# One product set for both comparison sides, five on-chip moves, and two copies in new places

## The chip, the cores and the metric

One core of a Trainium2 chip runs the whole program. The metric is the device time of one execution in microseconds (us). Five engines work side by side, each through its own list of instructions in order, and they wait for each other only by semaphores: TensorE (PE, matrix products into the eight PSUM banks), VectorE (DVE), ScalarE (ACT), GpSimd (POOL) and SyncE (SP), which here only issues transfers.

## The reference, cut to what matters

Eight sequences of 512 rows and 256 columns go through two layers. The first (causal attention with rotary positions beside an int8 projection) is not touched. The second is, for each of the eight sequences (a batch below):

```
xn    = layernorm(x)
left  = xn @ compare_left          # 256 -> 64
right = xn @ compare_right         # 256 -> 64
c     = left @ right.T / 16        # 512 x 512
g     = (c > threshold) * softmax(c + gate_bias)
attn  = g @ xn
xr, xk = two mixes of xn with xn moved down by one row, weights mu_r, mu_k
r     = sigmoid(xr @ W_r.T)
k     = square(relu(xk @ W_k.T))
out   = x + attn + r * (k @ W_v.T)
```

## The kernel before

Products are made in float16 pairs: a float32 value is split into a high part (its float16 copy) and a low part (what the copy left over), and three products, high by high, high by low and low by high, stand for one float32 product. Each split takes two passes: an engine copies (the high part), another subtracts (the low part).

The first layer runs as one long software pipeline over heads. The second runs batch by batch, as a pipeline written out by hand: each engine has a function `body3(n, u)` that lists its work of one turn, on batch n and on batches n+1 and n+2, and calls it for n = -1 to 7 (ACT from -2). The lists fix the order on each engine; nothing is scheduled at run time. One turn lasts some 20.6 us in the middle of the layer.

The work of a batch that the change touches or leans on, by function (engine, line):

- `turn` (PE, L1849): transposes the normalised rows `xn3` into banks 2 and 3. ACT copies them to `xt3h` (L940) and `xf3` (L947), DVE subtracts to `xt3l` (L1477).
- `rows_high` (ACT, L926, its instruction L932): copies the normalised rows, 128x1024, to float16 (`xn3h`). `rows_low` (POOL, L669, L674) subtracts to `xn3l`. Both are operands of the product `av3`. `rows_low(n+1)` is the first instruction of POOL's turn n; behind it stand `mix_before(n+1, 3)` (L683) and the two `key_low(n, .)` (L707), whose results `value(n, 0)` on PE waits for.
- `sides` (PE, L1859): six products of 512 columns for the left side into bank 2, and six for the right side into bank 3. The host lays each comparison matrix out twice, so that the result has the 64 values in partitions 0 to 63 and again in 64 to 127.
- `side_high` (ACT, L949, L955), twice: the left bank to `ls3`, the right bank to `rh3`. `side_low` (DVE, L1479): the lower half of `ls3` becomes the left side's low part (L1485), `rl3` the right side's (L1487). So `ls3` holds high over low, and two products (`ls3` by `rh3`, `ls3` by `rl3`) make a tile of comparisons.
- `compare` (PE, L1871): the four 128x512 tiles of comparisons, in banks 2 and 3 in turn. `top` (DVE, L1495) takes row maxima, `top_bias` (ACT, L963, L966) makes the bias, `exp3` (ACT, L974) the exponentials, `gated` (DVE, L1503, L1504) their reciprocals and the threshold mask.
- `pt3` (PE, L1926) transposes the masked tiles into banks 0 and 1, `pt3_high` (ACT, L983) and `pt3_low` (DVE, L1512) split them, `av3` (PE, L1943) multiplies them with the rows, `final` (DVE, L1542, four tiles) adds the result to `x_sb`, and SP stores it (L557).
- `mix_before` (POOL, L683) and `mix_all` (DVE, L1520) make the four mixes, `mix_high` (ACT, L991) and `mix_low` (POOL, L690) split them. `receptance`, `value` (PE, L1885) and `key` (PE, the products of L1650) use them; `key_relu`, `key_square`, `key_high` (ACT, L1006, L1014, L1022), `gate_value` (DVE, L1530) and `add_gated` (POOL, L697, L700) carry their results on.

The end of PE's turn n is: `key(n+1, 1)`, the two `sides(n+2, .)`, `pt3(n+1, 0)` and `(n+1, 1)`, `receptance(n+1, 1)`, `compare(n+2, 0)` and `(n+2, 1)`, `av3(n+1, 0)`, `pt3(n+1, 2)` and `(n+1, 3)`, `value(n+1, 0)`, `av3(n+1, 1)`; then the next turn begins with its two `turn`s, `value(n+1, 1)`, `receptance`, `compare` twice, `av3`, `key`, `av3`.

Of the kernel before, what the change touches and what calls it, by code (L numbers as in the profile page):

```python
# [5 lines left out]
NB = 8  # L6
SQ = 512
# [36 lines left out]
def build(nc, x_d, weights_d, w8_d, bqk_d, vec_d, thr_d, gate_d, tab_d, out_d):  # L44
# [11 lines left out]
    with ctx:  # L56
# [156 lines left out]
        kk = carve(KT * SQ).rearrange("p (k s) -> p k s", k=KT)  # L213
        st3 = sb("st3", [P, NT, 6], f32)
# [101 lines left out]
        lrl_done = sem("lrl_done")  # L316
        mixt_done = sem("mixt_done")
# [120 lines left out]
        def _(sp):  # L438
# [113 lines left out]

            for b in range(NB):
# [182 lines left out]
        def _(act):  # L736
# [189 lines left out]
            def rows_high(n, par):  # L926

                if absent3(n):
                    return
                after(act, xn3_done, made(NT, n, NT - 1))  # L930
                after(act, av3_mm, made(4, n - 2, 3))
                act.activation(xn3h[par], xn3[n % 2], ACT.Copy).then_inc(xn3h_done, 1)  # L932

            def xt_high(n, k):

                if absent3(n):
                    return
                after(act, tr3_mm, made(2, n, k))
                after(act, lr_mm, made(2, n - 1, 1))
                act.activation(xt3h[:, k, :], banks[2 + k][:], ACT.Copy).then_inc(xt3h_done, 1)  # L940
# [8 lines left out]
            def side_high(n, s):  # L949

                if absent3(n):
                    return
                after(act, lr_mm, made(2, n, s))
                after(act, c_mm, made(4, n - 1, 3))
                act.activation((ls3, rh3)[s], banks[2 + s][:], ACT.Copy).then_inc(lrh_done, 1)  # L955
# [68 lines left out]
            def body3(n, u):  # L1024
# [41 lines left out]
        def _(dve):  # L1066
# [412 lines left out]
            def side_low(n, s):  # L1479

                if absent3(n):
                    return
                after(dve, lrh_done, made(2, n, s))
                if s == 0:
                    dve.tensor_tensor(ls3[L:P], banks[2][L:P, :], ls3[L:P], ALU.subtract).then_inc(lrl_done, 1)  # L1485
                else:
                    dve.tensor_tensor(rl3, banks[3][:], rh3, ALU.subtract).then_inc(lrl_done, 1)  # L1487
# [59 lines left out]
            dve.memset(xf3[:, :, 0:1], 0.0).then_inc(xf3_zero, 1)  # L1547

            def body3(n, u):
# [10 lines left out]
                gate_value(n, 1, u)  # L1560
                gated(n + 1, 2, 1 - u)
# [18 lines left out]
            side_low(0, 0)  # L1580
            side_low(0, 1)
            top(0, 0, 0)
            mix_all(0, 2)
# [14 lines left out]
        def _(pe):  # L1598
# [260 lines left out]
            def sides(n, s, *users):  # L1859

                if absent3(n):
                    return
                after(pe, xt3l_done, made(2, n, 1))
                bank_free(users)
                pairs = []
                for k in range(KT):
                    a, z = lr_h[:, k, s, :], lr_l[:, k, s, :]
                    pairs += [(a, xt3h[:, k, :]), (a, xt3l[:, k, :]), (z, xt3h[:, k, :])]
                product(banks[2 + s][:], pairs, lr_mm)

            def compare(n, i, *users):  # L1871
# [3 lines left out]
                after(pe, lrl_done, made(2, n, 1))  # L1875
# [41 lines left out]
            def pt3(n, j, par):  # L1917
# [3 lines left out]
                if j == 0:  # L1921
                    after(pe, pm3_done, made(4, n, 3))
                    after(pe, x1_done, 2 * NB)
                after(pe, pt3l_done, made(4, n, j - 2))
# [29 lines left out]
            def body3(n, u):  # L1954

                turn(n + 2, 0, (pm3_done, 4, n + 1, 0), (lrl_done, 2, n + 1, 0), (pm3_done, 4, n, 2),
                     (xt3l_done, 2, n + 1, 0))
                turn(n + 2, 1, (pm3_done, 4, n + 1, 1), (lrl_done, 2, n + 1, 1), (pm3_done, 4, n, 3),
                     (xt3l_done, 2, n + 1, 1))
# [3 lines left out]
                compare(n + 1, 3, (xt3l_done, 2, n + 2, 1), (pm3_done, 4, n + 1, 1))  # L1963
                av3(n, 2, u)
# [6 lines left out]
                sides(n + 2, 0, (pm3_done, 4, n + 1, 2), (xt3l_done, 2, n + 2, 0))  # L1971
                sides(n + 2, 1, (pm3_done, 4, n + 1, 3), (xt3l_done, 2, n + 2, 1))
# [3 lines left out]
                compare(n + 2, 0, (lrl_done, 2, n + 2, 0))  # L1976
                compare(n + 2, 1, (lrl_done, 2, n + 2, 1))
# [18 lines left out]
            compare(0, 0, (lrl_done, 2, 0, 0))  # L1996
            compare(0, 1, (lrl_done, 2, 0, 1))
            attended(NB - 1, 1, (2, 3, 4, 5, 6, 7), pj)
# [51 lines left out]
```

## Time and profile before

| | us |
|---|---|
| median of 3 runs (lowest, highest) | 1029.79 (1029.18, 1029.96) |
| the profiled execution | 1030.44 |
| its span, first to last instruction | 1028.6 |
| PE busy | 987.3 (96%) |
| DVE busy | 837.6 (81%) |
| ACT busy | 757.0 (74%) |
| POOL busy | 767.6 (75%) |
| transfers' share of 16 DMA engines | 31% |

The span is the stretch that the profiler saw; the execution's own time is 1.84 us longer. A busy share is an average over both layers. The first layer ends near 840 us, and the stretch from there to the end is what the change touches. In a timeline a start and a duration are given for each instruction or run of like instructions; products overlap in PE's pipeline, so the distance from one start to the next, not the duration, is what an instruction costs there.

### The profile page before, as it was taken

The numbers are of one execution on the slowest core, as the hardware profiler recorded it, in microseconds if no ns is written. First come the engines' busy times: TensorE is split into PE (matmuls) and PEld (weight loads), VectorE is DVE, ScalarE is ACT, GpSimd is POOL, SyncE is SP. The second block draws the span as 40 slices with busy tenths as digits, with TensorE's granted clock in tenths as the row PEclk, the third lists the DMA queues.
The fourth block names the chain that finished last, engine by engine and source line by source line (L and its number), as shares of the span: only waits on it lengthen the run. The fifth ranks groups of instructions, "written<-read, shape, count | busy, mean of one in ns | idle before, by whom it ended". The sixth has DMA issues, their size and how long they took to land.

```text
span 1028.6 us, 23734 instructions
## 1 busy us (share of the span) xinstructions
PE 987.3 (96%) x8004; PEld 678.5 (66%) x8004; DVE 837.6 (81%) x2271; ACT 757.0 (74%) x2014; POOL 767.6 (75%) x942
## 2 busy tenths in 40 slices
PE   5889989999999999999999999999999998999997
PEld 4556655766666666666666666666666665777776
DVE  7989988788878888887778877778778756998875
ACT  5989987567676677676667667676766766999994
POOL 4777668877878787878687778787877545878874
PEclk9999999999999999999999999999999999999999
DMA  8734535234333333343333333333333100000101
GB/s 273 240 110 129 153 103 163 82 120 124 113 106 93 114 93 93 94 119 100 102 93 118 108 95 94 113 94 92 99 103 98 32 1 1 22 22 22 42 22 42
DMA packets 99704, 98.71 MB, mean 96 GB/s; under 512 B 13312, under 2 KB 95360, under 8 KB 98944
## 3 DMA queue, kind: packets, MB, share of 16 engines
q1 hardware_dynamic: 99584, 97.19, 31.0%
q8 instruction: 65, 1.06, 0.5%
q14 instruction: 55, 0.45, 0.2%
HBM read 56.25 MB, written 40.90 MB: 94 GB/s over the span
## 4 chain that ended last, share of the span: by engine, by line
PE 69%; DVE 15%; ACT 7%; issue 4%; POOL 3%; DMA 2%; SPq 0%; DVEq 0%; ACTq 0%; POOLq 0%
PE bank L1650 22%; PE bank L1747 12%; PE bank L1733 12%; PE bank L1764 7%; PE bank L1721 6%; PE bank L1722 5%; DVE arena L1361 2%; PE bank L1943 2%; ACT arena L872 2%; DVE arena L1520 2%; PE bank L1885 2%; POOL arena L628 2%; DVE arena L1377 1%; DMA arena<-in_weights 1%; DVE x_sb L1542 1%
## 5 line engine op out<-in xcount | busy, mean ns | idle before, releaser
L628 POOL TENSOR_SCALAR arena<-arena,rc 128x128 f32<-128x128 f32 (+3 forms) x512 | 277.7, 560 | 178.8 <-DVE rc L1370 177.9
L872 ACT ACTIVATE arena<-arena,nm 128x256 f32<-128x256 f32 (+3 forms) x512 | 283.5, 554 | 112.0 <-DVE nm L1361 107.5
L1361 DVE CUSTOM_DVE_ANT_0 arena<-bank,mask_rows 128x256 f32<-128x256 f32 (+3 forms) x512 | 232.8, 483 | 88.0 <-PE bank L1722 82.9
L1733 PE MATMUL bank<-ident,arena 128*128 128x128 f32 x1280 | 212.0, 278 | 12.4 <-DVE arena L1377 5.1
L1733 PEld LDWEIGHTS bank<-ident,arena 128*128 128x128 f32 x1280 | 149.8, 141 | 72.2 <-DVE arena L1377 29.8
L1722 PE MATMUL bank<-arena 128*128 128x256 f16 (+3 forms) x512 | 152.9, 299 | 0.0
L1747 PE MATMUL bank<-arena 128*64 128x512 f32 (+3 forms) x1024 | 152.0, 439 | 0.0
L1721 PE MATMUL bank<-arena 128*128 128x256 f16 (+3 forms) x512 | 139.9, 300 | 1.7 <-DMA arena<-scr 1.7
L1747 PEld LDWEIGHTS bank<-arena 128*64 128x64 f32 x1024 | 67.8, 136 | 94.8 <-issue 69.8
L1377 DVE COPY arena<-bank 128x512 f32<-128x512 f32 (+3 forms) x256 | 124.4, 486 | 3.7 <-PE bank L1733 3.3
L880 ACT ACTIVATE arena<-bank 128x512 f32<-128x512 f32 (+3 forms) x256 | 108.3, 423 | 15.1 <-PE bank L1733 14.4
L1650 PE MATMUL bank<-xsh,wh 128*128 128x512 f16 x256 | 97.2, 380 | 3.1 <-DVE wl L1203 2.4
L1764 PE MATMUL bank<-wh,arena 128*128 128x256 f16 x512 | 99.7, 273 | 0.4 <-DVE arena L1411 0.4
L1650 PE MATMUL bank<-xsh,wl 128*128 128x512 f16 x256 | 97.0, 379 | 0.0
L1650 PE MATMUL bank<-xsl,wh 128*128 128x512 f16 x256 | 97.0, 379 | 0.0
L890 ACT ACTIVATE arena<-bank,bvs 128x512 f16<-128x512 f32 x64 | 43.9, 687 | 71.5 <-PE bank L1747 71.3
L872 ACT ACTIVATION_READ_ACCUMULATOR arena<-arena,nm 128x1 f32 x512 | 96.1, 188 | 0.0
L1650 PE MATMUL bank<-wh,xsh 128*128 128x128 f16 x512 | 89.1, 219 | 1.7 <-DVE arena L1352 1.7
L1650 PE MATMUL bank<-wl,xsh 128*128 128x128 f16 x512 | 89.1, 219 | 0.0
L1650 PE MATMUL bank<-wh,xsl 128*128 128x128 f16 x512 | 89.1, 219 | 0.0
L600 POOL TENSOR_TENSOR arena<-arena 128x512 f32<-128x512 f32 x64 | 81.6, 1274 | 5.5 <-DVE arena L1352 5.4
L602 POOL TENSOR_TENSOR arena<-arena 128x512 f32<-128x512 f32 x64 | 83.0, 1297 | 0.0
(183 smaller groups left out, 2200.7 us busy)
## 6 DMA issues: line engine op xcount, KB each, us to landing
arena<-scr SPq DMA_DIRECT2D x320, 128.0 KB, 2.7
scr<-arena SPq DMA_DIRECT2D x256, 128.0 KB, 1.7
arena<-in_weights SPq DMA_DIRECT2D x5, 1024.0 KB, 7.7
x_sb<-in_x SPq DMA_DIRECT2D x8, 512.0 KB, 9.1
out<-x_sb SPq DMA_DIRECT2D x16, 256.0 KB, 2.2
xscr<-arena SPq DMA_DIRECT2D x12, 256.0 KB, 3.1
xsh<-xscr SPq DMA_DIRECT2D x6, 256.0 KB, 3.4
xsl<-xscr SPq DMA_DIRECT2D x6, 256.0 KB, 3.7
```

Source lines behind the costliest of these rows:

```text
L602: pool.tensor_tensor(r_o, t_es, t_oc, ALU.add).then_inc(r1_done, 1)
L628: last = pool.tensor_scalar(pr[slot][:, OFF[i]:OFF[i + 1]], pr[slot][:, OFF[i]:OFF[i + 1]], rc[:, slot, i:i + 1], 1.0, ALU.mult, ALU.mult)
L872: act.activation(pr[slot][:, OFF[i]:OFF[i + 1]], pr[slot][:, OFF[i]:OFF[i + 1]], ACT.Exp, scale=-1.0, bias=nm[:, slot, i:i + 1], accum_out ...
L880: act.activation(ptf[h][:, TOFF[j]:TOFF[j + 1]], (pt0, pt1)[h][:, 0:P * (NT - j)], ACT.Copy).then_inc(ptf_done[h], 1)
L1361: dve.tensor_tensor_reduce(pr[slot][:, OFF[i]:OFF[i + 1]], s_tile[i], mask_rows[:, SQ - P * (i + 1):SQ], -1.0, -MASKED, ALU.add, ALU.min, ...
L1377: dve.tensor_copy(ptf[1][:, TOFF[j]:TOFF[j + 1]], pt1[:, 0:P * (NT - j)]).then_inc(ptf_done[1], 1)
L1650: last = pe.matmul(out, lhs, rhs, start=(a == 0), stop=(a == len(pairs) - 1))
L1721: pe.matmul(out, q, kd[par][:, hh, 0:(i + 1) * P], start=True, stop=False)
L1722: last = pe.matmul(out, q, kz[par][:, hh, 0:(i + 1) * P], start=False, stop=True)
L1733: last = pe.transpose(banks[5 + h][:, (i - j) * P:(i - j + 1) * P], pr[2 * par + h][:, OFF[i] + j * P:OFF[i] + (j + 1) * P], ident[:])
L1747: last = pe.matmul(ob[h * L:(h + 1) * L, j * P:SQ], vf[:, j, h * L:(h + 1) * L], ptf[h][:, TOFF[j]:TOFF[j + 1]], start=(j == 0), stop=(j = ...
L1764: last = pe.matmul(bank[:, t * D:(t + 1) * D], o[:, slot, rows], w[:, p, :], start=(p == 0 and a == 0 and t == 0), stop=(p == NP - 1 and a ...
```

## The change: what it does

- **sides**: one set of six products takes the 128 weight columns that hold left and right once each, so that one bank has the left side in partitions 0 to 63 and the right side in 64 to 127. It goes to bank 0 (bank 2 for batch 0). On PE it moves from behind `key(n+1, 1)` to behind `compare(n+1, 3)`, ahead of `av3(n, 2)`.
- **side_high, side_low**: one instruction each on the whole bank, into two strips of dead weight space (`side_h`, `side_l`). On ACT `side_high(n+2)` now stands ahead of `top_bias(n+1, 1)`, on DVE `side_low(n+2)` ahead of `gated(n+1, 2)`.
- **move_sides**: SP moves the halves to where `compare` wants them, three transfers of 64 partitions behind `side_high` and two behind `side_low`. `compare` waits for all five. The lower half of `rl3` is set to zero once, so the product of the two low parts is left out.
- **rows_high**: the copy of the rows goes from ACT (behind `key_relu(n+1, 0)`) to DVE, behind `final(n, .)` and ahead of `mix_all(n+2, 2)`. POOL's list does not change.
- `pt3(n+1, 0)` also waits until `side_low(n+2)` has read bank 0; the start of the layer is reordered to match.

```diff
+            def move_sides(n):
+                after(sp, lrh_done, made(1, n))
+                for dst, src in ((ls3[0:L], side_h[0:L]), (rh3[0:L], side_h[L:P]), (rh3[L:P], side_h[L:P])):
+                    sp.dma_start(dst, src).then_inc(lr_moved, 16)
+                after(sp, lrl_done, made(1, n))
+                for dst, src in ((ls3[L:P], side_l[0:L]), (rl3[0:L], side_l[L:P])):
+                    sp.dma_start(dst, src).then_inc(lr_moved, 16)
+            move_sides(0)
+            move_sides(1)
             for b in range(NB):
+                move_sides(b + 2)
                 for u in range(2):
...
-                act.activation((ls3, rh3)[s], banks[2 + s][:], ACT.Copy).then_inc(lrh_done, 1)
+                after(act, lr_mm, made(1, n))
+                after(act, lr_moved, 80 * n)
+                act.activation(side_h, banks[0 if n else 2][:], ACT.Copy).then_inc(lrh_done, 1)
...
ACT body3:
                     normalised(n + 3, (0, 1))
+                side_high(n + 2)
                 top_bias(n + 1, 1, 1 - u)
                 exp3(n + 1, 2, 1 - u)
                 exp3(n + 1, 3, 1 - u)
                 key_relu(n + 1, 0)
-                rows_high(n + 2, u)
                 key_square(n + 1, 0)
                 key_high(n + 1, 0)
-                side_high(n + 2, 0)
                 key_relu(n + 1, 1)
-                side_high(n + 2, 1)
...
+            def rows_high(n, par):            # now on DVE
+                after(dve, xn3_done, made(NT, n, NT - 1))
+                after(dve, av3_mm, made(4, n - 2, 3))
+                dve.tensor_copy(xn3h[par], xn3[n % 2]).then_inc(xn3h_done, 1)
+            def side_low(n):
+                after(dve, lrh_done, made(1, n))
+                dve.tensor_tensor(side_l, banks[0 if n else 2][:], side_h, ALU.subtract).then_inc(lrl_done, 1)
...
DVE body3:
                 gate_value(n, 1, u)
+                side_low(n + 2)
                 gated(n + 1, 2, 1 - u)
                 gated(n + 1, 3, 1 - u)
                 mix_all(n + 2, 0)
                 mix_all(n + 2, 1)
                 final(n, 0, u)
                 final(n, 1, u)
+                rows_high(n + 2, u)
                 mix_all(n + 2, 2)
-                side_low(n + 2, 0)
-                side_low(n + 2, 1)
                 pt3_low(n + 1, 0)
...
+            lr_hf = wh[:, C_LR:C_WR].rearrange("p (k c) -> p k c", k=KT)[:, :, L:3 * L]
+            def sides(n, *users):
...
                 for k in range(KT):
+                    pairs += [(lr_hf[:, k], xt3h[:, k, :]), (lr_hf[:, k], xt3l[:, k, :]), (lr_lf[:, k], xt3h[:, k, :])]
+                product(banks[0 if n else 2][:], pairs, lr_mm)
             def compare(n, i, *users):
-                after(pe, lrl_done, made(2, n, 1))
+                after(pe, lr_moved, 80 * (n + 1))
...
PE body3:
                 compare(n + 1, 3, (xt3l_done, 2, n + 2, 1), (pm3_done, 4, n + 1, 1))
+                sides(n + 2, (pt3l_done, 4, n, 2))
                 av3(n, 2, u)
                 key(n + 1, 0, (er_done, 2, n + 1, 0))
...
                 key(n + 1, 1, (y3a_done, 2, n, 1))
-                sides(n + 2, 0, (pm3_done, 4, n + 1, 2), (xt3l_done, 2, n + 2, 0))
-                sides(n + 2, 1, (pm3_done, 4, n + 1, 3), (xt3l_done, 2, n + 2, 1))
                 pt3(n + 1, 0, 1 - u)
...
start of the layer, PE:
-            sides(0, 0, (xt3l_done, 2, 0, 0))
-            sides(0, 1, (xt3l_done, 2, 0, 1))
+            sides(0, (xt3l_done, 2, 0, 0))
             attended(NB - 1, 0, (4, 5, 6, 7), wo)
-            attended(NB - 1, 1, (0, 1), pj)
+            attended(NB - 1, 1, (0, 1, 2, 3), pj)
             compare(0, 0, ...)
```

## Rows read from the trace of the kernel before

**Rows 1.** Windows: start:end, length, then busy us (instructions) by engine, clock, DMA.

```profile
952.42:973.00 20.58, 20.40 (x154) 15.02 (x153) 16.97 (x32) 19.45 (x40) 16.91 (x16) 1.00 0.08 27
```

**Rows 2.** Timeline of PE: start us, duration us, line, operation, out<-in, count.

```profile
880.13 1.04 PE L1856 MATMUL bank<-ident,arena 128*128 128x128 f32 x8
881.00 0.38 PE L1885 MATMUL bank<-wh,arena 128*128 128x256 f16 x2
...
884.49 1.47 PE L1943 MATMUL bank<-arena 128*128 128x256 f16 x12
885.80 0.59 PE L1650 MATMUL bank<-arena,wh 128*128 128x512 f16 x2
...
950.25 0.59 PE L1650 MATMUL bank<-arena,wh 128*128 128x512 f16 x2
...
954.14 1.03 PE L1926 MATMUL bank<-ident,arena 128*128 128x128 f32 x8
...
959.62 0.38 PE L1885 MATMUL bank<-wh,arena 128*128 128x256 f16 x2
```

**Rows 3.** Timeline of ACT in the same stretch.

```profile
954.34 0.60 ACT L955 ACTIVATE arena<-bank 128x512 f16<-128x512 f32 x1
954.83 1.08 ACT L983 ACTIVATE arena<-bank 128x512 f16<-128x512 f32 x2
...
967.99 0.39 ACT L963 ACTIVATE arena<-nm,gate,sc_c 128x2 f32<-128x2 f32 x1
...
968.74 0.78 ACT L974 ACTIVATE arena<-bank,arena,sc_c 128x512 f32<-128x512 f32 x1
...
971.07 1.06 ACT L932 ACTIVATE arena<-arena 128x1024 f16<-128x1024 f32 x1
```

**Rows 4.** Timeline of DVE: a pair of mixes alone, and one turn.

```profile
888.92 1.40 DVE L1520 SCALAR_TENSOR_TENSOR arena<-arena,vec 128x512 f32<-128x512 f32 x2
...
952.42 1.65 DVE L1542 SCALAR_TENSOR_TENSOR x_sb<-bank,arena,x_sb 128x256 f32<-128x256 f32 x4
954.00 1.05 DVE L1520 SCALAR_TENSOR_TENSOR arena<-arena,vec 128x512 f32<-128x512 f32 x1
...
956.41 1.28 DVE L1512 TENSOR_TENSOR arena<-bank,arena 128x512 f16<-128x512 f32 x2
...
970.40 0.17 DVE L1503 RECIPROCAL arena<-arena 128x1 f32<-128x1 f32 x1
...
971.12 1.95 DVE L1520 SCALAR_TENSOR_TENSOR arena<-arena,vec 128x512 f32<-128x512 f32 x2
```

**Rows 5.** Timeline of POOL; in brackets idle before, and what ended it.

```profile
951.93 2.56 POOL L674 TENSOR_TENSOR arena<-arena 128x1024 f16<-128x1024 f32 x1
...
957.17 1.16 POOL L707 TENSOR_TENSOR arena<-arena 128x512 f16<-128x512 f32 x1 [0.43 <-ACT arena L1022]
...
968.04 1.36 POOL L683 TENSOR_SCALAR arena<-arena,omu 128x512 f32<-128x512 f32 x2
```

**Rows 6.** Groups of DVE by line and form: count, busy us, mean ns, idle before.

```profile
L1394 DVE TENSOR_TENSOR arena<-xsh,xsl 128x1024 f32<-128x1024 f16 x8 | 9.6, 1194 | 0.0
...
L1405 DVE TENSOR_SCALAR arena<-arena 128x1024 bf16<-128x1024 f32 x8 | 5.5, 688 | 0.0
```

**Rows 7.** All instructions of L674: ns least/median/most, first and last start us.

```profile
L674 POOL TENSOR_TENSOR arena<-arena x8: 2126/2560/2564, 850.0 to 993.1; 128x1024 f16<-128x1024 f32 x8
```

**Rows 8.** Timeline of PE: an early idle, and one at the layer's start.

```profile
28.93 0.38 PE L1650 MATMUL bank<-xsh,wh 128*128 128x512 f16 x1 [1.85 <-DVE wl L1203]
...
859.73 1.64 PE L1856 MATMUL bank<-ident,arena 128*128 128x128 f32 x8 [1.65 <-DVE arena L1504]
```

**Rows 9.** Windows just behind it, columns as in Rows 1.

```profile
862.00:864.00 2.00, 2.00 (x11) 1.37 (x9) 0.90 (x2) 1.04 (x4) 0.91 (x1) 0.50 0.00 0
```

**Rows 10.** The page's DMA issues: count, KB each, us from issue to landing.

```profile
arena<-scr SPq DMA_DIRECT2D x320, 128.0 KB, 2.7
```

**Rows 11.** Timeline of SP: two issues in the first layer.

```profile
798.01 0.90 SPq L515 DMA_DIRECT2D arena<-scr  x2
```

More of the change, by code:

```diff
@@ L924, in _ @@
                 ring(n)
[L926 to L932, printed above, removed]
             def xt_high(n, k):
@@ L938, in xt_high @@
                 after(act, tr3_mm, made(2, n, k))
-                after(act, lr_mm, made(2, n - 1, 1))
+                after(act, lr_mm, made(1, n - 1))
                 act.activation(xt3h[:, k, :], banks[2 + k][:], ACT.Copy).then_inc(xt3h_done, 1)
@@ L947, in xt_whole, with side_high @@
                 act.activation(xf3[:, k, 1:SQ + 1], banks[2 + k][:], ACT.Copy).then_inc(xf3_done, 1)
[L949 removed]
+            def side_high(n):
                 if absent3(n):
                     return
[L953 to L955 removed]
+                after(act, lr_mm, made(1, n))
+                after(act, lr_moved, 80 * n)
+                act.activation(side_h, banks[0 if n else 2][:], ACT.Copy).then_inc(lrh_done, 1)
             def top_bias(n, p, par):
@@ L1477, in xt_low3 @@
                 dve.tensor_tensor(xt3l[:, k, :], banks[2 + k][:], xt3h[:, k, :], ALU.subtract).then_inc(xt3l_done, 1)
-            def side_low(n, s):
+            def rows_high(n, par):
                 if absent3(n):
                     return
[L1483 to L1487, printed above, removed]
+                after(dve, xn3_done, made(NT, n, NT - 1))
+                after(dve, av3_mm, made(4, n - 2, 3))
+                dve.tensor_copy(xn3h[par], xn3[n % 2]).then_inc(xn3h_done, 1)
+            def side_low(n):
+                if absent3(n):
+                    return
+                after(dve, lrh_done, made(1, n))
+                dve.tensor_tensor(side_l, banks[0 if n else 2][:], side_h, ALU.subtract).then_inc(lrl_done, 1)
             def top(n, p, par):
@@ L1547, in _ @@
             dve.memset(xf3[:, :, 0:1], 0.0).then_inc(xf3_zero, 1)
+            dve.memset(rl3[L:P], 0.0).then_inc(rl3_zero, 1)
             def body3(n, u):
@@ L1579, in _ @@
             mix_all(0, 1)
-            side_low(0, 0)
-            side_low(0, 1)
+            side_low(0)
+            mix_all(0, 2)
+            rows_high(0, 0)
             top(0, 0, 0)
-            mix_all(0, 2)
             residual(NB - 1, 0, wo)
@@ L1857, in turn @@
                 last.then_inc(tr3_mm, 1)
-            def sides(n, s, *users):
+            lr_hf = wh[:, C_LR:C_WR].rearrange("p (k c) -> p k c", k=KT)[:, :, L:3 * L]
+            lr_lf = wl[:, C_LR:C_WR].rearrange("p (k c) -> p k c", k=KT)[:, :, L:3 * L]
+            def sides(n, *users):
                 if absent3(n):
@@ L1923, in pt3 @@
                     after(pe, x1_done, 2 * NB)
+                if j == 0 and not absent3(n + 1):
+                    after(pe, lrl_done, made(1, n + 1))
                 after(pe, pt3l_done, made(4, n, j - 2))
@@ L1954, in body3 @@
             def body3(n, u):
[L1956 to L1959, printed above, removed]
+                turn(n + 2, 0, (pm3_done, 4, n + 1, 0))
+                turn(n + 2, 1, (pm3_done, 4, n + 1, 1))
                 value(n, 1, (er_done, 2, n, 1))
@@ L1975, in body3 @@
                 receptance(n + 1, 1, (kr_done, 2, n + 1, 1))
-                compare(n + 2, 0, (lrl_done, 2, n + 2, 0))
-                compare(n + 2, 1, (lrl_done, 2, n + 2, 1))
+                compare(n + 2, 0, (pm3_done, 4, n + 1, 2))
+                compare(n + 2, 1, (pm3_done, 4, n + 1, 3))
                 av3(n + 1, 0, 1 - u)
```

19 lines of the change are left out of this document (13 added, 6 removed).

## The prediction

> **What bounds the kernel now.** I read the page's busy shares first (PE 96%), then the windows of the second layer one turn at a time, then each engine's timeline of one clean turn. In the turn from 952.42 to 973.00 us PE is busy 20.40 of 20.58 us, ACT 19.45, DVE 16.97, POOL 16.91 [rows 1]. PE is the bound, but by little: ACT has 1.1 us of air, and DVE and POOL, with 3.6 us each, sit in chains that reach PE only just in time. So a product set taken away is worth its time only if the chains that feed PE shorten with it. Those chains, not the busy shares, decide this change. The layer has six turns (n = 0 to 5) with all of the changed work, and its start.
>
> **What is removed.** A set of six products of 512 columns costs 1.30 us of PE: three such sets (a key and the two old sides) run from 950.25 to 954.14 [rows 2]. One set a batch goes: 8 x 1.30 = 10.4 us, if nothing takes its place. ACT loses one side copy (0.60) and the copy of the rows (1.06) a batch [rows 3]. On DVE the two old subtractions stood between the third mix and `pt3_low`, from 954.00 + 1.05 to 956.41, 1.36 us [rows 4]; one of some 0.7 us comes back in a place where DVE waits for the exponentials anyway, so I count it at nothing.
>
> **What is added.** (a) Five transfers of 64 partitions. The first layer's, of 128 KB, land 2.7 us after issue [rows 10] and are issued 0.45 us apart [rows 11]. In the turn worked out below, counted from `turn(n+2, 1)`, `side_high` ends at 6.0 and `side_low` 0.7 later, the last move is issued at 7.7 and lands at 10.4; `compare(n+2, 0)` comes at 12.6 at the earliest (5.23, five sets of 1.30 to 1.31: `av3`, `key`, `av3`, `key`, `receptance`, and the two `pt3` at 0.87). PE's queue behind that wait holds `av3(n+1, 0)` and the rest of the turn, but there are 2.2 us of cover, and I count it at nothing. SP's stores stand behind the moves of batch n+2, which are issued some 4 us before `final(n)` ends; they lose nothing. (b) The zeroing of half of `rl3`, once: a fraction of a microsecond beside a DVE that waits. (c) The copy of the rows on DVE. No such copy stands in the trace. The nearest row is a one-input pass over 1024 columns from float32 to a 16-bit type, 0.69 us; the other end is the two-input pass over 1024 columns, 1.19 us [rows 6]. I take 0.69, since the copy too has one input, and keep 1.19 for the range.
>
> **What is moved, and why it costs.** This is the point of the change that decides. The copy of the rows is not only work for DVE: POOL's `rows_low` waits for it, and behind `rows_low` on POOL stand `mix_before` and the two `key_low`, for which `value(n+1, 0)` on PE waits. Before, ACT had the copy done early (971.07 + 1.06 = 972.13, before POOL was free at 972.50), and the key's low part was ready at 957.17 + 1.16 = 958.33 for a `value` that began at 959.62 [rows 2, 3, 5]: 1.3 us of slack. Now the copy stands on DVE behind the mask of the last exponential, two mixes and four tiles of `final`. And the exponentials themselves now stand behind `side_high`, which waits for the new product set. That closes a loop through four engines. I add it up from the issue of `turn(n+2, 1)` on PE to that of `turn(n+3, 1)`:
>
> - PE: half of a pair of `turn`s, 0.44 (the pair takes 881.00 - 880.13 = 0.87); `value`, `receptance` and two `compare`s, 884.49 - 881.00 = 3.49; the new set 1.30 [rows 2]. Now 5.23.
> - ACT: `side_high` starts 0.20 behind PE's last product (954.34 against the next group's 954.14) and the next instruction 0.49 later [rows 2, 3]; now 5.92. The maxima have long been there (both `compare`s are through at 4.1, two maxima at 0.6 each give 5.4 at most), so `top_bias` starts. 0.75 to the third exponential, and 970.40 - 968.74 = 1.66 until DVE can mask the fourth [rows 3, 4]. Now 8.33.
> - DVE: the mask 0.72 (to 971.12); two mixes, `final` 1.58 (954.00 - 952.42) and the copy 0.69 [rows 4, 6]. The two mixes took 1.95 in the last turn, with POOL at work, and 1.40 alone; 0.08 of each overlaps what follows, so 1.87 or 1.32 [rows 4]. In the new order POOL is through with its list by about 8.7 and stands idle, waiting for the copy; I take 1.32. Now 12.64.
> - POOL: `rows_low` 2.56, the median (least 2.13) [rows 7]; one `mix_before` 0.68 (two took 1.36) and two `key_low` of 1.16 [rows 5]. With 0.05 at the hand-over, now 18.25.
> - PE: `value` and `av3` at 1.31 each (884.49 to 885.80), half a pair of `turn`s 0.44 [rows 2]. The loop closes at 21.3 us.
>
> PE's own work in a turn falls from at most 20.4 to 19.1 [rows 1], so it would stand still over 2 us a turn: first at `av3(n+1, 0)`, which it could begin at 13.5 (the 12.6 of its `compare`s and 0.87 for the two), while its `pt3_low` ends behind the copy and the third mix, at 12.6 + 1.05 + 0.68 = 14.3; then well over a microsecond at `value(n+1, 0)`. What is late next, if the POOL part were gone, is that same `pt3_low`, in a loop of some 19.6. So each of the six turns takes 21.3 instead of 20.58: +0.7 us each, +4.3 in all. The start gains: before the first `turn(1, .)` one set less stands ahead of the last first-layer products, whose residual the first mask waits for, so 1.3 us come off, and the first POOL chain keeps that gain (its turn had a slack of that size). The last turns have neither sides nor a copy and stay. Sum: 4.3 - 1.3 = +3.0 us on the profiled execution's 1030.44, which is 1033.4; that execution lies 0.65 above the median of the runs, so the median comes to **1033 us**.
>
> **A rule weighed against this.** The two mixes show what sharing costs: 1.95 beside a busy POOL, 1.40 beside an idle one [rows 4]; `rows_low` shows it from the other side, 2.13 or 2.56 [rows 7]. The Trainium skill (SBUF - State Buffer, on the port that VectorE and GpSimd share) says that a VectorE instruction with two SBUF inputs, or in a two-port mode, holds the shared port pair for its whole length and the other engine blocks fully. The trace agrees in size, an extra 0.43 to 0.55 us being most of one mix of 0.7 us. By that rule the third mix, issued right behind the copy, would be first at the port and `rows_low` would end after 0.7 + 2.13 us; by the row it is 2.56. The loop would be 21.5 by the rule against 21.3.
>
> **Rivals.**
> 1. *The same loop, and the clock falls in its stalls.* PE idled 1.65 us before 859.73, and its `turn`s then took 1.64 us in place of 1.04; behind them it ran at a granted clock of 0.50, the lower of its two levels (1.2 GHz), in the window to 864 [rows 2, 8, 9]. At half speed the sets of such a stretch cost twice as much: 1.31 more for one, and I count 1.7 us for each such fall. Stalls of 0.8 and over 1 us would come each turn. Against: an idle of 1.85 us before 28.93 [rows 8] left the clock at full, as did every other one of the trace. If it falls in three to six of the turns, +5 to +10 more: 1038 to 1043, nominal 1040.
> 2. *Faster: the chains overlap more than I think, and PE keeps the set's time.* If the `value` wait does not bind (the copy is issued early, or POOL's list runs ahead), the loop left is PE's own, 19.1 at most. Eight sets give up to 10.4: 1019.4, and 1024 if half of it is lost again in ACT's order. For it: ACT, the second busiest, loses 1.66 us a turn. Against: every link of the sum above is forced by the written order.
> 3. *No change:* the short ends throughout, `rows_low` 2.13, gives a loop of 20.85, +0.3 a turn, and 1030.3 with the start's gain; or one link of half a microsecond hidden. 1028 to 1032.
> 4. *The moves are late.* Only beyond 2.2 us of cover, and then PE's stalls at `av3` and `value` absorb two more; a landing of over 7 us would be needed. Each further microsecond costs 6. I give it 2 in 100 and fold it into the first.
>
> **How the numbers follow.** The forecast (the loop at full clock) 0.50; its own range is 1030 to 1041: the low end with `rows_low` at 2.13, the high end with the copy at 1.19, mixes at 1.87 and a `mix_before` beside a mix, 22.5 a turn. The clock rival 0.20, faster 0.17, no change 0.13. Range for 8 in 10: 1022 to 1042, which leaves out the best part of the faster case and the worst of the clock. Within 0.2% is what a measurement of this kernel can't tell from none, 2.06 us, 1027.7 to 1031.9: the no-change case and the forecast's low end, 0.18. Faster 0.18, slower 0.64.
>
> **What would show it.** In the new profile: the distance between two groups of `final` 21.3 instead of 20.6 us in six turns; PE waiting 1 to 2 us before `value`'s L1885 line, released by POOL's `key_low`; POOL idle 3 to 4 us before `rows_low`, released by DVE's copy; that copy at 0.69; transfers landed before `compare`. The prediction is wrong if `key_low` is done before `value` comes up, if the copy takes well over 1.2 us, if PE waits for a transfer, or if a turn falls below 20 us.

## The result, and the profile after

| | before | after |
|---|---|---|
| median of the runs, us | 1029.88 (1029.18 to 1030.99, 4 runs) | 1036.91 (1035.74 to 1038.96, 4 runs) |
| the profiled execution, us | 1030.44 | 1038.96 |
| its span, us | 1028.6 | 1037.1 |
| PE busy, us (share of the span) | 987.3 (96%) | 982.8 (95%) |

The ratio is 1.0067, interval 1.0047 to 1.0088: slower by 7.0 us. The forecast was 1033, range 1022 to 1042.

The time went into the turns. The first fence has windows of the new kernel's trace from one group of `final` to the next, columns as in [rows 1]; the three short windows below them are stretches in which PE's clock was low, two inside these turns and one in the turn behind them.

```profile
890.43:913.39 22.96, 20.89 (x148) 15.47 (x146) 17.80 (x39) 17.98 (x37) 16.08 (x15) 0.93 0.13 39
913.39:935.62 22.23, 19.61 (x148) 14.34 (x146) 20.60 (x37) 17.99 (x37) 16.01 (x15) 1.00 0.14 39
935.62:958.58 22.96, 20.89 (x148) 15.17 (x146) 20.78 (x38) 17.98 (x37) 16.03 (x15) 0.93 0.13 38
958.58:979.88 21.30, 19.24 (x148) 14.38 (x146) 16.20 (x31) 17.98 (x37) 16.08 (x15) 1.00 0.15 42
...
900.00:902.00 2.00, 2.00 (x12) 1.38 (x11) 1.83 (x3) 0.00 (x0) 1.58 (x3) 0.50 0.04 8
944.00:946.00 2.00, 2.00 (x11) 1.36 (x10) 1.90 (x6) 0.61 (x2) 1.52 (x2) 0.50 0.00 0
989.00:991.00 2.00, 2.00 (x11) 1.42 (x10) 1.01 (x2) 0.00 (x0) 1.00 (x2) 0.50 0.00 0
```

A clean turn takes 21.30 us and has 19.24 us of PE work in it, against 20.58 and 20.40 in [rows 1]. Three of the six take 22.96 with the clock at 0.93 on average (the third of them starts at 979.88), one takes 22.23 at full clock, and two are clean. At 900, 944 and 989 us PE runs at a granted clock of 0.50, its lower level of 1.2 GHz. Now the clean turn, DVE first (timeline, columns as in [rows 4]):

```profile
975.56 0.69 DVE L1500 TENSOR_TENSOR wh<-bank,wh 128x512 f16<-128x512 f32 x1 [0.27 <-ACT wh L965]
977.07 0.16 DVE L1516 RECIPROCAL arena<-arena 128x1 f32<-128x1 f32 x1 [0.81 <-ACT arena L984]
977.83 0.16 DVE L1516 RECIPROCAL arena<-arena 128x1 f32<-128x1 f32 x1
978.56 1.41 DVE L1533 SCALAR_TENSOR_TENSOR arena<-arena,vec 128x512 f32<-128x512 f32 x2
979.88 1.65 DVE L1555 SCALAR_TENSOR_TENSOR x_sb<-bank,arena,x_sb 128x256 f32<-128x256 f32 x4
981.45 0.68 DVE L1493 CAST arena<-arena 128x1024 f16<-128x1024 f32 x1
982.05 0.74 DVE L1533 SCALAR_TENSOR_TENSOR arena<-arena,vec 128x512 f32<-128x512 f32 x1
982.71 1.28 DVE L1525 TENSOR_TENSOR arena<-bank,arena 128x512 f16<-128x512 f32 x2
```

The copy of the rows (the CAST of L1493) takes 0.68 us, behind the mixes and `final`. What waits for it stands in POOL's and PE's timelines of the same turn:

```profile
982.22 2.56 POOL L692 TENSOR_TENSOR arena<-arena 128x1024 f16<-128x1024 f32 x1 [4.12 <-DVE arena L1493]
984.76 0.69 POOL L701 TENSOR_SCALAR arena<-arena,omu 128x512 f32<-128x512 f32 x1
985.42 2.26 POOL L725 TENSOR_TENSOR arena<-arena 128x512 f16<-128x512 f32 x2
987.74 0.39 PE L1905 MATMUL bank<-wh,arena 128*128 128x256 f16 x2 [1.93 <-POOL arena L725]
```

POOL stands idle for 4.12 us until the copy comes, then runs `rows_low` (2.56), `mix_before` and two `key_low`, and PE has stood idle 1.93 us when `value(n+1, 0)` can start. In the kernel before, `key_low` was ready 1.3 us before PE wanted it [rows 2, 5]. The view of PE's waits, from 880 to 1000 us (in total, times, longest), shows this as the only wait of weight:

```profile
PE bank L1905 <- POOL arena L725: 9.7, 5, 1.9
PE bank L1870 <- DVE arena L1517: 0.5, 1, 0.5
```

The transfers are not among them. The page's line that answers to [rows 10] is

```profile
arena<-wh SPq DMA_DIRECT2D x40, 64.0 KB, 2.0
```

**The account.** From `value(0, 0)` to `value(6, 0)`, six turns, the new kernel takes 133.7 us and the old one 123.2. The 10.5 us are six turns at 21.30 (127.8, so +4.6), three falls of the clock at 1.66 each (22.96 - 21.30; +5.0), and 0.93 for the turn of 22.23. The rest of the profiled execution's +8.5 is the first layer, which the change does not touch and which ended 1.6 us later in this execution, the start (-1.1 to the first `turn(1, .)`, and -1.0 behind it, where the old kernel had its one fall of the clock, [rows 9], and the new one has none), and -1.5 in the last turns. I don't count the 1.6 us of the first layer to the change. PE waits there for a transfer just ahead of 46 us, in every trace of this case and for 1.12 to 3.43 us (1.67 before, 2.35 in the changed kernel), and in five of the fourteen (the changed kernel and experiments 1, 5, 9 and 11) its clock then falls to 0.50; in experiments 7 and 8 it falls behind the next wait, near 55 us, and in the kernel before at neither. In these seven the second layer's first DVE instruction starts at 843.7 us or later, in the other seven at 843.5 or earlier, but for experiment 12 (844.8), whose wait was 3.28 us.

### The profile page after: what moved, and what is told of

Read it like the earlier page. It is cut to its first block, busy times and chain, and to the rows that moved or that the text cites. A ratio compares the mean times of both kernels' runs of the same rounds, so it can differ in the third digit from the quotient of the medians.

```text
span 1037.1 us, 23654 instructions
## 1 busy us (share of the span) xinstructions
PE 982.8 (95%) x7956; PEld 675.2 (65%) x7956; DVE 837.3 (81%) x2272; ACT 745.7 (72%) x1998; POOL 763.4 (74%) x942
## 4 chain that ended last, share of the span: by engine, by line
PE 67%; DVE 12%; POOL 7%; ACT 6%; issue 5%; DMA 2%; SPq 0%; POOLq 0%; DVEq 0%; ACTq 0%
PE bank L1664 20%; PE bank L1761 12%; PE bank L1747 11%; PE bank L1778 7%; PE bank L1735 6%; PE bank L1736 5%; DVE arena L1369 2%; PE bank L1905 2%; PE bank L1965 2%; POOL arena L646 2%; POOL arena L692 1%; DVE arena L1385 1%; ACT arena L890 1%; POOL arena L725 1%; DMA scr<-arena 1%
## 5 line engine op out<-in xcount | busy, mean ns | idle before, releaser
L898 ACT ACTIVATE arena<-bank 128x512 f32<-128x512 f32 (+3 forms) x256 | 108.5, 424 | 14.9 <-PE bank L1747 14.3
L1778 PE MATMUL bank<-wh,arena 128*128 128x256 f16 x512 | 99.7, 273 | 0.9 <-DVE arena L1419 0.9
```

Source lines behind the costliest of these rows:

```text
L898: act.activation(ptf[h][:, TOFF[j]:TOFF[j + 1]], (pt0, pt1)[h][:, 0:P * (NT - j)], ACT.Copy).then_inc(ptf_done[h], 1)
L1778: last = pe.matmul(bank[:, t * D:(t + 1) * D], o[:, slot, rows], w[:, p, :], start=(p == 0 and a == 0 and t == 0), stop=(p == NP - 1 and a ...
```

## Experiments

Each is compared with the kernel before on the same chip. "The changed kernel" is the one measured above.

**1. The copy alone, in the kernel before.**

```
  (ACT)                 key_relu(n + 1, 0)
-                       rows_high(n + 2, u)
  (DVE)                 final(n, 1, u)
+                       rows_high(n + 2, u)
                        mix_all(n + 2, 2)
```

> The kernel before with nothing changed but the copy of the rows, on DVE behind final. Theory (the copy's place and side_high ahead of the exponentials each add a part to the loop): the fourth exponential is masked 7.6 us after turn(., 1), not 8.3, but the mixes run beside a busy POOL, so the loop is 20.6 to 21.2 against 20.6: 1030 to 1034. Rival (the copy's place costs it all by itself): 1036 or more.

Measured: 1034.47 us (1031.96 to 1035.61), ratio 1.0039, interval 1.0025 to 1.0053. Three turns took 20.81 to 20.93 us, two 22.3. PE waited at three places, each only a little:

```profile
PE bank L1857 <- DVE arena L1503: 1.8, 2, 0.9
PE bank L1651 <- DVE arena L1486: 1.5, 5, 0.4
PE bank L1886 <- POOL arena L707: 1.1, 5, 0.2
```

So one line's move from ACT to DVE costs, with all the old products in place, over half of the change's loss (0.39% of 0.67%). The two long turns were expected by neither theory; they wait 0.9 us at `turn` for a mask (first line), and experiments 4 and 5 are about them.

**2. The change without the copy's move.**

```
  (ACT)                 key_relu(n + 1, 0)
+                       rows_high(n + 2, u)
                        key_square(n + 1, 0)
  (DVE)                 final(n, 1, u)
-                       rows_high(n + 2, u)
```

> The changed kernel with the copy of the rows back on ACT, behind key_relu(n+1, 0); all else as changed. Theory (the loop sides, side_high, exponentials, copy, rows_low, key_low, value sets the turn): POOL gets the copy 2.7 us earlier, value no longer waits for key_low, and a turn falls from 21.3 to 19.2 to 19.6 us, bound by PE and by pt3_low; with no long stall the clock stays at full. 1036.9 - 6 x 1.8 - about 5 for the clock: 1019 to 1023. Rival (the cost is in side_high ahead of the exponentials or in the transfers, not in the copy's place): at least 1032.

Measured: 1026.12 us (1025.42 to 1027.14), ratio 0.9962, interval 0.9947 to 0.9977: 10.8 us below the changed kernel, and faster than before. PE waits for POOL nowhere, the clock stays at 1.00, and the turns take 20.24 to 20.55 us, not the 19.2 to 19.6 expected. It lies between the two ranges expected. That the POOL chain carries the loss is shown; why a turn is still 1.0 us over PE's work is the matter of experiments 6 to 10.

**3. The copy on DVE, but ahead of the two mixes.**

```
  (DVE)                 gated(n + 1, 3, 1 - u)
+                       rows_high(n + 2, u)
                        mix_all(n + 2, 0)
                        ...
                        final(n, 1, u)
-                       rows_high(n + 2, u)
```

> The changed kernel with the copy still on DVE but ahead of mix_all(n+2, 0), so before two mixes and final. Same work on every engine. Theory (what counts is when the copy ends, not which engine makes it): the copy can start when av3(n, 3) is through, 2.4 us earlier than now; POOL's chain is then no longer last, pt3_low is, and a turn takes 19.6 us: 1021 to 1025. Rival (DVE's load is what costs): unchanged, 1035 to 1039.

Measured: 1039.03 us (1037.54 to 1039.78), ratio 1.0085, interval 1.0070 to 1.0100. A clear miss of the theory, by 14 us and in sign. The number is at the edge of the rival's (DVE's load, 1035 to 1039), but DVE has the same instructions as in the changed kernel; what is new is what they meet. The copy starts 9.9 us behind the pair of `turn`s in place of 12.4, so 2.5 us earlier, but now `rows_low` meets the two mixes (timeline):

```profile
978.58 0.69 DVE L1493 CAST arena<-arena 128x1024 f16<-128x1024 f32 x1 [0.28 <-PE bank L1965]
979.18 3.30 DVE L1533 SCALAR_TENSOR_TENSOR arena<-arena,vec 128x512 f32<-128x512 f32 x2
979.36 2.58 POOL L692 TENSOR_TENSOR arena<-arena 128x1024 f16<-128x1024 f32 x1 [1.16 <-DVE arena L1493]
982.40 1.65 DVE L1555 SCALAR_TENSOR_TENSOR x_sb<-bank,arena,x_sb 128x256 f32<-128x256 f32 x4
985.37 1.98 PE L1965 MATMUL bank<-arena 128*128 128x256 f16 x12 [2.39 <-DVE arena L1525]
```

The pair of mixes takes 3.30 us in place of 1.41, `final` and `pt3_low` come later by that, and PE waits 2.39 us at `av3(n+1, 0)`. Turns alternate between 21.45 us and, with a fall of the clock, 23.11. The rule that the forecast weighed (the Trainium skill, "SBUF — State Buffer", section "Who interferes with whom") speaks of an exclusive lock on the port that VectorE and GpSimd share; the trace agrees in size, since the excess of 1.89 us is most of a `rows_low` (2.13 at the least, [rows 7]). In the order of the changed kernel the same `rows_low` meets one mix at most, and that is 0.74 us.

**4. Spare products in the stall, and 5. the same with the roots moved.** Experiment 4 puts eight products of 512 columns, which nobody reads, ahead of `value(n+1, 0)`. Experiment 5 adds the edit below. `roots` are small DVE instructions (128x8) that take the inverse square root of the last two batches' variances, six at the end of each of two turns.

```
  (PE)                  pt3(n + 1, 3, 1 - u)
+                       keep_busy(n + 1)
                        value(n + 1, 0, (kr_done, 2, n + 1, 0))
  (DVE, experiment 5)   side_low(n + 2)
+                       if 1 <= n < 3:
+                           roots(last_two, 3, (2 * n - 2, 2 * n - 1))
                        gated(n + 1, 2, 1 - u)
                        ...
-               elif n < 3:
-                   roots(last_two, 3, (2 * n - 2, 2 * n - 1))
```

> The changed kernel with eight spare products of 512 columns (1.73 us, results thrown away) on PE in the place of its wait for key_low, in the turns that have the wait. Theory (the clock falls in some turns because PE stands still 1.93 us): no half-clock stretch any more, turns of 21.3 us throughout, 1031 to 1033.5. Rival (the long turns of 22.96 us have another cause): 1036 to 1039 as before.

> Base: the changed kernel with the spare products ahead of value (which keeps the clock at full rate), and in addition the root of the last two batches' variances taken not at the end of two turns, beside POOL's rows_low and key_low, but ahead of gated(n+1, 2), where DVE waits for the exponentials and POOL has no long pass. My theory (the two long turns, 22.23 and 22.30 us, come from these small DVE instructions, 1.0 us each beside POOL, which delay the next mask): all five turns 21.3, 1.9 us less than the filled kernel, 1033 to 1034 us. Rival (the two turns are long for another reason, or the instructions take as long in the new place): 1035 to 1036.

Experiment 4: 1035.50 us (1034.16 to 1035.84), ratio 1.0053, interval 1.0036 to 1.0070, with turns of 21.30, 22.23, 22.30, 21.30 and 21.30. The windows of three of them:

```profile
889.46:910.76 21.30, 20.96 (x156) 15.15 (x154) 17.79 (x40) 17.98 (x37) 16.09 (x15) 1.00 0.14 42
910.76:932.99 22.23, 21.34 (x156) 15.08 (x154) 20.60 (x38) 17.99 (x37) 16.01 (x15) 1.00 0.14 39
932.99:955.29 22.30, 21.33 (x156) 15.06 (x154) 20.67 (x38) 17.99 (x37) 16.02 (x15) 1.00 0.14 40
```

The loop is not shortened by the filling, and the clock stays at 1.00 throughout: the 22.96 turns were 21.30 plus what a fall costs behind a stall. (This is the fastest of four executions; the other three have a mean clock of 0.998, as the kernel before has with one fall, wherever it lies. Experiment 5's trace, filled too, has one fall in the first layer and none in the second.) The time stayed 2 us above what was expected, and two turns are 1.93 us longer together. In them DVE is busy 20.6 to 20.7 us, against 17.8 in the first line and 16.2 in the two that are not shown. DVE's timeline of the changed kernel shows what these hold, and that of the kernel before the same instructions:

```profile
919.03 1.08 DVE L1090 TENSOR_SCALAR nw<-nw 128x8 uint32<-128x8 uint32 x1
920.15 1.08 DVE L1092 TENSOR_SCALAR nw<-nw 128x8 int32<-128x8 int32 x1
921.26 1.01 DVE L1097 TENSOR_TENSOR nw<-nw 128x8 f32<-128x8 f32 x1
922.30 1.01 DVE L1099 SCALAR_TENSOR_TENSOR nw<-nw 128x8 f32<-128x8 f32 x1
923.35 0.17 DVE L1101 SCALAR_TENSOR_TENSOR nw<-nw 128x8 f32<-128x8 f32 x1
```

```profile
918.19 1.01 DVE L1082 TENSOR_SCALAR nw<-nw 128x8 uint32<-128x8 uint32 x1
919.24 0.17 DVE L1084 TENSOR_SCALAR nw<-nw 128x8 int32<-128x8 int32 x1
919.44 0.17 DVE L1089 TENSOR_TENSOR nw<-nw 128x8 f32<-128x8 f32 x1
```

An instruction on eight columns takes 0.17 us while POOL is idle and 1.0 to 1.1 us beside one of POOL's two-input passes of 512 columns; two pairs of such passes end at 921.20 and 923.29, and the second and the fourth of the long instructions 0.03 us or less behind them. Since POOL's list now runs later, four meet it in place of one, and the next mask is late.

Experiment 5: 1036.39 us (1034.96 to 1037.87), ratio 1.0053, interval 1.0032 to 1.0073: not the 1033 to 1034 hoped for. The turns took 23.00, 22.98 and three times 21.30. The extra time moved by one turn, together with the roots, so the roots are its cause. But ahead of `gated(n+1, 2)` there was no room either: they take 2.6 us there (931.02 to 933.64; two of the six still meet a pass of POOL, against what was expected), of which DVE's wait for the exponential hides 0.8 to 0.9, and 1.7 is seen.

**6 and 7. What holds the kernel of experiment 2: is it the wait for the sides?** Its turns of 20.3 us I put down to ACT's list, which waits 0.50 us for the sides. Both kernels start from experiment 2; in 6 the sides are split behind the exponentials again, in 7 DVE makes `side_high`.

```
  (ACT, 6)  -           side_high(n + 2)
                        top_bias(n + 1, 1, 1 - u)
                        exp3(n + 1, 2, 1 - u)
                        exp3(n + 1, 3, 1 - u)
            +           side_high(n + 2)
  (DVE, 6)  side_low(n + 2) behind gated(n + 1, 3, 1 - u)
  (DVE, 7)  +           side_high(n + 2)
                        side_low(n + 2)
```

> Base: the changed kernel with the copy of the rows back on ACT; and the sides split behind the exponentials again (side_high behind exp3(n+1, 3), side_low behind gated(n+1, 3)), the single product set and the transfers kept. Theory: what bounds the kernel with the copy on ACT (turns of 20.3 us) is ACT's own list with its 0.50 us of waiting for the sides; without that wait turns of 19.8 and 1023 to 1024 us. Rival: the sides come too late for the comparison (side_low behind the masks ends at 9 us, the moves land 2 us and their issues later, comparison at 12.6 with nothing to spare) or pt3 waits for the split, and the turn stays at 20.3 or more: 1026 or above.

> Base: the changed kernel with the copy of the rows back on ACT; and side_high (512 columns, 0.60 us) made by DVE right ahead of side_low instead of by ACT ahead of the exponentials. Theory (ACT's list with its wait for the sides sets the turn of 20.3 us): ACT loses 0.60 us and the wait of 0.50, DVE has 1.3 us of idle time at that place; turns of 19.3 to 19.5 and 1020 to 1022 us. Rival (DVE's masks come later by 0.6 us and with them the mixes, final and PE's receptance): turns of 20 to 20.3, 1025 to 1026.

Measured: 1025.92 us (1025.04 to 1026.95), ratio 0.9952, interval 0.9937 to 0.9967; and 1027.04 (1025.81 to 1027.71), ratio 0.9960, interval 0.9947 to 0.9973. Both have the turns of experiment 2 (20.24 to 20.60), and both the same wait of PE, six times 0.9 us, here that of experiment 6:

```profile
PE bank L1904 <- ACT arena L1024: 5.3, 6, 0.9
PE bank L1869 <- DVE arena L1518: 0.6, 2, 0.3
```

So my theory fell. L1904 is `receptance(n+1, 1)`, L1024 `key_relu(n+1, 1)`. In these kernels it costs nothing to split the sides ahead of the exponentials, nor does it matter which engine does it: the three ratios, 0.9962, 0.9952 and 0.9960, lie in each other's intervals.

**8, 9 and 10. The relu directly behind the copy.** Edit of 8, on experiment 2; 9 is the same on experiment 7, 10 on experiment 6.

```
  (ACT)                 rows_high(n + 2, u)
+                       key_relu(n + 1, 1)
                        key_square(n + 1, 0)
                        key_high(n + 1, 0)
-                       key_relu(n + 1, 1)
```

> Base: the changed kernel with the copy of the rows back on ACT (turns 20.3 us; PE waits 0.89 us in each at receptance(n+1, 1) for key_relu(n+1, 1)). Here key_relu(n+1, 1) stands directly behind the copy, ahead of the square and the high part of key 0. New theory: with the product set gone, the bound is a short loop av3(n, 3) on PE - copy of the rows (waits 0.54 to 0.68 for it) - square, high, relu on ACT - receptance on PE; it does not pass the sides, since moving or splitting them elsewhere left 0.89 us of that wait. With the relu 1.2 us earlier the wait goes and av3(n+1, 0) is the next, waiting 0.2 for its pt3_low: turns of 19.5 to 19.7, 1021 to 1023 us. Rival (ACT's list, 18.7 busy of 20.3, with its waits for PE sets the turn): the wait moves elsewhere, 1025 to 1026.

> As the kernel with the relu directly behind the copy, and side_high made by DVE ahead of side_low. Theory of the PE-ACT loop: PE-bound in both, so 0 to 0.3 us a turn better at most: 1020 to 1022 us. Rival (ACT's list bounds once the relu is early): this one is 0.5 to 1 us a turn faster than the one with side_high on ACT ahead of the exponentials, 1018 to 1020.

> As the kernel with the relu directly behind the copy, and the sides split behind the exponentials (side_high behind exp3(n+1, 3), side_low behind gated(n+1, 3)). This tells what splitting the sides ahead of the exponentials costs by itself once nothing else holds the turn: if the exponentials' wait for the sides (0.50 us on ACT) matters, this one is 0.3 to 0.5 us a turn faster, 1019 to 1021 us; if not, the two are within 0.1 us a turn, 1021 to 1023.

Measured: 1028.89 us (ratio 0.9987, interval 0.9976 to 0.9999), 1029.48 (0.9990, 0.9980 to 0.9999) and 1027.89 (0.9982, 0.9971 to 0.9993): some 3 us slower than without the edit, where 3 to 7 faster were expected. Experiments 8 and 10, which differ only in where the sides are split, are equal within their intervals. All three have turns of 20.5 to 20.6 us. Between experiments 2 and 8 that is only 1.0 us over the five middle turns; another 1.3 us lie in the last two, whose cause was not followed. The wait at `receptance` is gone, and the same time is waited at `turn` for the mask of the first exponential. The timeline of experiment 8, cut to the links of one turn:

```profile
951.30 1.06 ACT L950 ACTIVATE arena<-arena 128x1024 f16<-128x1024 f32 x1 [0.54 <-PE bank L1964]
959.79 0.78 ACT L992 ACTIVATE arena<-bank,arena,sc_c 128x512 f32<-128x512 f32 x1
960.69 0.16 DVE L1517 RECIPROCAL arena<-arena 128x1 f32<-128x1 f32 x1 [3.17 <-ACT arena L992]
961.65 1.39 PE L1869 MATMUL bank<-ident,arena 128*128 128x128 f32 x8 [0.87 <-DVE arena L1518]
970.26 1.47 PE L1964 MATMUL bank<-arena 128*128 128x256 f16 x12
971.83 1.06 ACT L950 ACTIVATE arena<-arena 128x1024 f16<-128x1024 f32 x1 [0.54 <-PE bank L1964]
```

Read in order of time it is a loop: the copy of the rows on ACT waits for `av3(n, 3)`, whose buffer it overwrites; from the copy ACT takes 9.4 us to the first exponential, DVE 1.0 us to its mask, and PE 10.2 us from `turn` to the next `av3(n, 3)`. The sum is 20.53 us, the turn. The timelines show 0.18 us of waiting within ACT's 9.4 us and none within PE's 10.2. Without the edit the loop is another through the same copy, in experiment 2's timeline:

```profile
969.54 1.06 ACT L950 ACTIVATE arena<-arena 128x1024 f16<-128x1024 f32 x1 [0.54 <-PE bank L1964]
971.69 0.67 ACT L1024 ACTIVATE arena<-bank,sc 128x512 f32<-128x512 f32 x1
972.50 0.38 PE L1904 MATMUL bank<-wh,arena 128*128 128x256 f16 x2 [0.89 <-ACT arena L1024]
```

It takes 2.96 us from the copy through square, high part and relu to `receptance`, and the other 17.3 of its 20.24 us are PE's, from there to the next `av3(n, 3)`. Both contain PE's new product set, which the change put ahead of `av3(n, 2)`; in the old order it stood behind `key(n+1, 1)`, outside the part from `turn` to `av3(n, 3)`. So the 1.3 us that PE saves a turn seem to be partly outside the loops that bind: that is read from the order and the traces, and no run isolates it. Whether another place for the set, or a third buffer for the copy, would free them was not tried.

**11. Experiment 7 with the roots of experiment 5.**

> The changed kernel with the copy of the rows on ACT, side_high on DVE, and the roots of the last two batches ahead of gated(n+1, 2). Theory: as the kernel with side_high on DVE, and up to 1 us less, if that one has turns lengthened by the roots at their old place; 1019 to 1022 us. Rival: DVE has no room left ahead of gated(n+1, 2) in those two turns, so it is 0 to 1 us slower than without the move.

Measured: 1035.43 us (1031.99 to 1037.35), ratio 1.0043, interval 1.0027 to 1.0058: 8 us slower than without the roots' move, where 1 was the worst expected. Falls of the clock are in this too: two of the eight executions take 1032.0 us at a mean clock of 0.998, the others 1035.2 to 1037.4 at 0.993 to 0.997. The masks, later by the roots, push the mixes into `rows_low` (DVE's and POOL's timelines):

```profile
913.04 2.13 POOL L692 TENSOR_TENSOR arena<-arena 128x1024 f16<-128x1024 f32 x1 [1.41 <-ACT arena L950]
913.53 3.29 DVE L1533 SCALAR_TENSOR_TENSOR arena<-arena,vec 128x512 f32<-128x512 f32 x2
```

3.29 us for the pair again, as in experiment 3, and turns of 24.8 and 22.9.

**12. Ten transfers in place of five,** on experiment 2: each move is issued a second time, to memory that nobody reads, and `compare` waits for all.

```
-  for dst, src in ((ls3[0:L], side_h[0:L]), (rh3[0:L], side_h[L:P]), (rh3[L:P], side_h[L:P])):
+  for dst, src in (..., (spare(0), side_h[0:L]), (spare(1), side_h[L:P]), (spare(2), side_h[L:P])):
...
-                after(pe, lr_moved, 80 * (n + 1))
+                after(pe, lr_moved, 160 * (n + 1))
```

> Base: the changed kernel with the copy of the rows back on ACT (1026.1 us); and each of the five transfers of a batch is issued twice, the second time to spare memory that nobody reads, and the comparison waits for all ten. This prices the transfers. The five last transfers more take some 0.6 us each on SP's queue, 2.5 to 3 us in all, against a cover that I put at 2.2 us for the first five: if the cover is of that size, PE waits 0 to 0.8 us a turn at compare(n+2, 0) and the time is 1026 to 1030 us; if the transfers already were at the edge, 3 us a turn more, 1040 or above; if the cover is larger, no change, 1026.

Measured: 1032.72 us (1030.72 to 1033.94), ratio 1.0023, interval 1.0012 to 1.0033; 6 us above experiment 2 by the ratios. By the two traces 4.7 us of it are at two places of the start, and 0.6 in one late turn. The two places:

```profile
858.63 1.89 PE L1667 MATMUL bank<-arena 128*128 128x512 f16 x4 [3.16 <-DMA wh<-wh]
879.06 1.04 PE L1667 MATMUL bank<-arena 128*128 128x512 f16 x4 [0.53 <-DMA wh<-wh]
```

The first is `compare(0, 0)`, followed by a fall of the clock (1.89 us for four products in place of 1.04). The turns of 20.3 to 20.6 us are those of experiment 2, but for one of 20.84 with a wait of 0.9. The five spare moves take 3.1 us of SP's queue (1.87 and 1.24), and in five turns of six `compare` does not wait even so: the cover there is 3 us, with the 0.9 that PE waits at `receptance`, against 2.2 in the forecast. The thin place is the first batch, which the forecast didn't look at: in the changed kernel the last of its moves goes out between 852.8 and 853.4 us, lands 2.0 us after it was issued, and `compare(0, 0)` starts at 854.90. In experiments 7, 9 and 11, where DVE splits the first sides behind two mixes, PE waits 1.4 us for the moves there.

## Why the prediction was right, and where it wasn't

The direction and the mechanism were right. The size was not: slower by 3 us was forecast and 7.0 us was measured, and 1036.9 lies nearer to the clock rival's 1038 to 1043 than to 1033. The loop itself has the size given; what is missing are the falls of the clock, which stood in a rival, and a term that the sum doesn't have.

- **The loop of 21.3 us a turn** was right to the digit: 21.30, with the mask, mixes (1.41), `final`, copy (0.68) and POOL's list as summed: from the issue of `turn(n+2, 1)`, `rows_low` starts at 12.70 (forecast 12.69) and `value` at 18.22 (18.25). The forecast's other sum, 21.5 us, let `rows_low` start only behind the third mix. It starts 0.17 us behind the mix's start, so only the rest of the mix adds to its 2.13, and it takes 2.56. The copy has the duration of the one-input pass chosen, not the 1.19 kept as its upper end. Experiment 2 takes out the copy's move and with it 10.8 us.
- **The clock.** The rival, with a chance of 0.20, said falls in three to six turns at 1.7 us each. The profiled execution has three, at 1.66, and the traces of the two filled kernels (experiments 4 and 5) have none, so it is the stalls that bring them. Both cases of the forecast happened, the second in part. What the falls cost the median is less sure. The four runs take 1038.96, 1035.84, 1035.74 and 1037.99 us at mean clocks of 0.993, 0.996, 0.998 and 0.995. The first has four falls, one of them in the first layer, and the kernel before has 0.998 with one; by that I estimate two, one and three falls for the others, in either layer. The ratio of experiment 4, 1.0053 against 1.0067, puts the falls behind these stalls at some 1.4 us of the median, by intervals that overlap. What decides which turns fall is open; the wait before `value` is 1.93 us in both kinds.
- **A term left out:** the roots on DVE, +0.93 and +1.00 in two turns (experiments 4 and 5; in the profiled execution a fall of the clock covers the second). With the forecast's +3.0 and the clock's 1.4 this makes 6.3 of the 7.0 us, as an estimate. The forecast treated the six turns as alike. It had read one clean turn, and the odd ones differ by instructions that last 0.17 us beside an idle POOL.
- **The start.** Forecast -1.3, measured -1.1 to the first `turn(1, .)`. The zeroing, counted at nothing, stands ahead of the last products of the first layer, where PE waits 0.89 us for DVE at L1778, 0.44 before. On DVE that product's input starts 0.49 us behind the layer's first memset, with the 0.27 us of zeroing between them, and 0.03 us before, so the forecast's "beside a DVE that waits" looks wrong; no run left the zeroing out.
- **PE's first stall** at `av3(n+1, 0)` was forecast at 0.8 us and is 0.3: the mix ahead of `pt3_low` took 0.74, not 1.05, so `pt3_low` was there at 13.9 of the turn and not at 14.3. The stall at `value` absorbs it either way.
- **Transfers, one `side_low`, SP's stores:** nothing, right in the turns; for the first batch right with next to nothing to spare.
- **The faster rival** (1019 to 1024) names a condition that is needed and not enough. When the `value` wait doesn't bind, as in experiments 2, 6 and 7, the kernel is faster than before, but by 4 us, not 6 to 10: "PE keeps the set's time" fails on the loops through the copy's buffer.

The best versions measured leave the copy of the rows on ACT: the change with that alone (1026.12 us, 0.9962 of before), and with the sides split behind the exponentials too (1025.92, 0.9952). They are equal within the measurement.

## What to carry to other kernels

When work moves between engines, add up the loop from one issue of the bounding engine to its next, through every engine that the moved result passes; a busy share of 81% (DVE) or 75% (POOL) says nothing about the room at the new place. Removed work on the bounding engine is a gain only in the loops that contain it, and here, as the traces are read above, the gain went first into a wait for a copy and, with that undone, into a buffer that is read until late. Then look at the turns that are not alike: the first, and those with a few tiny instructions more.

## What the runs showed of the hardware

- A DVE instruction on 128x8 elements takes 0.17 us beside an idle POOL and 1.0 to 1.1 us beside a two-input POOL pass of 512 columns (experiment 4). A pair of two-input mixes takes 1.41 us alone and 3.30 beside `rows_low` (experiment 3). So a single small instruction can wait as long as a large one.
- Stalls of 1.93 us were followed by a PE clock of 0.50 in three turns of six, each for some 3.4 us, at a price of 1.66 us. The same stall left it at 1.00 in the others, as did the 1.85 us of [rows 8].
- The length of a single stall did not decide it here. At one and the same wait of the first layer (ahead of 46 us, fourteen traces) the clock fell behind 1.96, 2.04, 2.35, 2.94 and 3.43 us, and stayed at 1.00 behind nine others from 1.12 to 3.28 us, with 1.93 and 2.36 among them.
- A transfer of 64 KB within the state buffer lands in 2.0 us, and its issue takes 0.6 us of SP's queue.
